# Scores of two heads on 64 rows each, and units taken in pairs, in the masked attention of a four-layer kernel

## The reference, cut to what matters

```python
def _masked_attention(xf, Wq, Wk, Wv, lookahead):
    q = jnp.einsum('bnd,hed->bhne', xf, Wq)
    k = jnp.einsum('bnd,hed->bhne', xf, Wk)
    v = jnp.einsum('bnd,hed->bhne', xf, Wv)
    scale = 1.0 / jnp.sqrt(jnp.asarray(q.shape[-1], q.dtype))
    s = jnp.einsum('bhqe,bhke->bhqk', q, k) * scale
    n = s.shape[-1]
    i = jnp.arange(n)
    mask = i[:, None] <= i[None, :] if lookahead else i[:, None] >= i[None, :]
    s = jnp.where(mask, s, jnp.finfo(s.dtype).min)
    p = jax.nn.softmax(s, axis=-1)
    return jnp.einsum('bhqk,bhke->bhqe', p, v)

o_lb = _masked_attention(xf, Wq_lb, Wk_lb, Wv_lb, lookahead=False)
o_la = _masked_attention(xf, Wq_la, Wk_la, Wv_la, lookahead=True)
o = jnp.concatenate([o_lb, o_la], axis=1)
out = jnp.einsum('bnd,od->bno', o.reshape(B, T * F, D), Wo)
```

## Time and profile before

| | |
|---|---|
| time, median of 3 runs (lowest, highest) | 1525.02 us (1522.62, 1526.16) |
| span of the profiled execution | 1518.8 us |
| PE busy | 1399.6 us, 92% of the span |
| DVE, ACT, POOL busy | 700.1, 390.7, 527.4 us |
| mean granted TensorE clock | 0.969 of full |
| one step of a pair in the second layer, looking back | 48.57 us |
| the same, looking ahead | 49.04 us |

### The profile page before, as it was taken

How to read it: one execution, slowest core, us unless ns; L and a number is a source line. 1 busy time by engine, 2 the same in 40 slices (tenths; PEclk the granted TensorE clock), 3 DMA queues, 4 the chain that set the end, 5 groups by cost and what they waited for, 6 DMA issues and landing times. The chain is left out here.

```text
span 1518.8 us, 20095 instructions
## 1 busy us (share of the span) xinstructions
PE 1399.6 (92%) x7344; PEld 1090.4 (72%) x7344; DVE 700.1 (46%) x1399; ACT 390.7 (26%) x941; POOL 527.4 (35%) x491
## 2 busy tenths in 40 slices
PE   4899799779999999999888999999999999795998
PEld 3678665358888877888666778777877787574787
DVE  6214423775345412455436555455234645558322
ACT  2311112043223301233201333233013322305322
POOL 3444298023332285223247322322442222144000
PEclk9899999899999999999989999999999999896999
DMA  4111052001111022111012101101110010000012
GB/s 172 42 42 42 28 85 36 0 28 40 38 32 31 28 76 63 35 28 35 28 42 82 35 22 35 29 27 27 42 41 28 28 35 28 15 28 3 0 35 77
DMA packets 36748, 59.63 MB, mean 39 GB/s; under 512 B 4848, under 2 KB 13840, under 8 KB 36688
## 3 DMA queue, kind: packets, MB, share of 16 engines
q1 hardware_dynamic: 35120, 55.42, 13.3%
q10 hardware_dynamic: 1568, 3.38, 0.6%
HBM read 50.40 MB, written 4.19 MB: 36 GB/s over the span
## 5 line engine op out<-in xcount | busy, mean ns | idle before, releaser
L127 POOL TENSOR_TENSOR w_hi<-w_raw,zeros 128x512 fp32r<-128x512 f32 x168 | 216.8, 1291 | 765.6 <-PE PS L151 731.8
L151 PE MATMUL PS<-xh,w_hi 128*128 128x512 f32 x960 | 332.9, 421 | 26.7 <-ACT xh L292 13.7
L151 PE MATMUL PS<-xl,w_hi 128*128 128x512 f32 x960 | 310.0, 397 | 3.0 <-DVE xl L286 2.7
L151 PE MATMUL PS<-xh,w_lo 128*128 128x512 f32 x960 | 309.4, 396 | 0.0
L129 POOL TENSOR_TENSOR w_lo<-w_raw,w_hi 128x512 fp32r<-128x512 f32 x168 | 220.1, 1310 | 13.2
L151 PEld LDWEIGHTS PS<-xh,w_hi 128*128 128x128 f32 x960 | 173.8, 192 | 69.5 <-issue 26.1
L151 PEld LDWEIGHTS PS<-xl,w_hi 128*128 128x128 f32 x960 | 181.8, 190 | 47.4 <-DVE xl L286 6.9
L151 PEld LDWEIGHTS PS<-xh,w_lo 128*128 128x128 f32 x960 | 182.9, 191 | 41.0
L1013 ACT ACTIVATE prob<-PS,nmax 128x256 f32<-128x256 f32 (+1 forms) x256 | 112.1, 443 | 229.3 <-DVE nmax L1142 114.9
L1154 DVE TENSOR_SCALAR prob<-prob,prec 128x256 f32<-128x256 f32 (+1 forms) x256 | 113.5, 485 | 4.5
L151 PE MATMUL PS<-oh,w_hi 128*128 128x512 f32 x256 | 93.4, 406 | 5.6 <-DVE ol L1087 3.7
(11 more groups left out here) (149 smaller groups left out, 1980.6 us busy)
## 6 DMA issues: line engine op xcount, KB each, us to landing
w_raw<-in_w SPq DMA_DIRECT2D x168, 256.0 KB, 2.6
A<-G SPq DMA_DIRECT2D x32, 128.0 KB, 4.5
out_x<-xT SPq DMA_DIRECT2D x16, 256.0 KB, 2.1
xT<-in_x SPq DMA_DIRECT2D x4, 512.0 KB, 8.3
xT<-in_x ACTq DMA_DIRECT2D x4, 512.0 KB, 8.7
ET<-in_emb ACTq DMA_DIRECT2D x1, 961.0 KB, 13.3
ka<-in_hot SPq DMA_DIRECT2D x2, 192.0 KB, 4.0
c<-in_c SPq DMA_DIRECT2D x1, 192.0 KB, 2.5
```

Of the source, the lines that this page charges most:

```text
L127: pool.tensor_tensor(w_hi[:, s, :], w_raw[:, s, :], zeros[:, :], ALU.add).then_inc(w_hi_done, 1)
L151: m = nc.tensor.matmul(PS[:, banks[h], :], wt[:, slot, w], x[:, c, h * HALF:h * HALF + HALF], start=first and k == 0, stop=last and k == 2)
```

## The change

The scores of both heads of an image are issued together, by a new function `scores_of_both`: for each of the two query blocks and each of the three products one matmul on rows 0 to 63 for the first head and one on rows 64 to 127 for the second, in turns, into bank S and bank S+1; then the four mask matmuls over all 128 rows, two into each bank, after which each bank's unit is reported. The queries have no padding and no planes any more: one ACT and one DVE instruction of 128 partitions each fill `qh` and `ql`, and the four memsets are gone.

The order in which PE goes through the units is new as well (`heads_in_pairs`). Before, scores and transposes alternated unit by unit. Now it is, for each image: scores of both heads, a chunk of v, transposes of the previous image's first head, a chunk of v, transposes of its second head, and outputs two images back. As both score banks are written at once, the scores of an image wait until ACT has taken the exponentials of both heads of the image before (`p_exp`). On DVE the first group of outputs leaves PSUM after unit 6 rather than 5. ACT's order keeps as it was.

```diff
@@ query tiles, evacuation on ACT and DVE
-            qh = sb(ctx, "qh", [P, 2, T], F32R)
-            ql = sb(ctx, "ql", [P, 2, T], F32R)
+            qh = sb(ctx, "qh", [P, T], F32R)
+            ql = sb(ctx, "ql", [P, T], F32R)
...
-                        for hh in range(2):
-                            rows = slice(64 * hh, 64 * hh + 64)
-                            last = nc.scalar.activation(qh[rows, hh, :], PS[rows, 0:2, :].rearrange("p a n -> p (a n)"), ACT.Copy)
-                        last.then_inc(q_evac, 1)
+                        nc.scalar.activation(qh[:, :], both, ACT.Copy).then_inc(q_evac, 1)
...
-                    if c in (4, 5) and masked:
-                        t = (qh, ql)[c - 4]
-                        nc.vector.memset(t[64:P, 0, :].bitcast(F32), 0.0)
-                        nc.vector.memset(t[0:64, 1, :].bitcast(F32), 0.0).then_inc(zeroed, 1)
...
-                        if u == 5:
+                        if u == (6 if masked else 5):
                             evac_o(j, int(ahead), 0)
@@ scores on PE
-                            for i, (x, y) in enumerate(((qh, kh), (qh, kl), (ql, kh))):
-                                nc.tensor.matmul(PS[:, S + u % 2, at + lo:at + hi], x[:, hh, qs], y[:, ks],
-                                                 start=i == 0, stop=False)
+                def scores_of_both(j, b, ahead):
+
+                    if b:
+                        pe.wait_ge(p_exp, 8 * j + 2 * b)
+                    for qt, (lo, hi) in enumerate(spans(ahead)):
+                        at = qt * N
+                        qs, ks = slice(b * N + qt * P, b * N + qt * P + P), slice(b * N + lo, b * N + hi)
+                        for i, (x, y) in enumerate(((qh, kh), (qh, kl), (ql, kh))):
+                            for hh in range(2):
+                                rows = slice(64 * hh, 64 * hh + 64)
+                                nc.tensor.matmul(PS[:, S + hh, at + lo:at + hi], x[rows, qs], y[rows, ks],
+                                                 start=qt == i == 0, stop=False, skip_group_check=True)
+                    for hh in range(2):
+                        for qt in range(2):
+                            at = qt * N + qt * P
+                            m = nc.tensor.matmul(PS[:, S + hh, at:at + P], identb[:, :], maskb[:, int(ahead), :],
+                                                 start=False, stop=True, skip_group_check=True)
+                        m.then_inc(s_done, 1)
@@ the order of the units on PE
+                def heads_in_pairs(j, ahead, more, next_v, second_half):
+                    for b in range(B):
+                        if b == 0 or b == 2 and not more:
+                            halves = 2 if more or b else 1
+                            pe.wait_ge(k_evac, 2 * j + halves)
+                            pe.wait_ge(split_done, 2 * j + halves)
+                        scores_of_both(j, b, ahead)
+                        if b == 0:
+                            next_v(1)
+                            next_v(2)
+                            second_half(range(0, 6))
+                            pe.wait_ge(v_ready, j + 1)
+                        else:
+                            next_v(2 * b + 1)
+                            if b == 1:
+                                second_half(range(6, CK))
+                            transposed(j, 2 * b - 2, ahead)
+                            if b < 3:
+                                next_v(2 * b + 2)
+                            transposed(j, 2 * b - 1, ahead)
+                            if b >= 2:
+                                outputs(j, 2 * b - 4, ahead)
+                    if not more:
+                        for u in (6, 7):
+                            transposed(j, u, ahead)
+                            outputs(j, 2 * u - 8, ahead)
```

More of the change, by code:

```diff
@@ L1091, in take_q @@
                     if masked:
-                        for hh in range(2):
-                            rows = slice(64 * hh, 64 * hh + 64)
-                            last = nc.vector.tensor_tensor(ql[rows, hh, :], PS[rows, 0:2, :].rearrange("p a n -> p (a n)"),
-                                                           qh[rows, hh, :].bitcast(F32), ALU.subtract)
-                        last.then_inc(qa_evac, 1)
+                        nc.vector.tensor_tensor(ql[:, :], PS[:, 0:2, :].rearrange("p a n -> p (a n)"), qh[:, :].bitcast(F32),
+                                                ALU.subtract).then_inc(qa_evac, 1)
                     else:
@@ L1226, in scores @@
                         qs, ks = slice(b * N + qt * P, b * N + qt * P + P), slice(b * N + lo, b * N + hi)
-                        if not masked:
-                            m = nc.tensor.matmul(PS[:, S + u % 2, at + lo:at + hi], q[:, hh, qs], k[:, hh, ks],
-                                                 start=True, stop=True)
-                        else:
-                            for i, (x, y) in enumerate(((qh, kh), (qh, kl), (ql, kh))):
-                                nc.tensor.matmul(PS[:, S + u % 2, at + lo:at + hi], x[:, hh, qs], y[:, ks],
-                                                 start=i == 0, stop=False)
-                            m = nc.tensor.matmul(PS[:, S + u % 2, at + qt * P:at + qt * P + P], identb[:, :],
-                                                 maskb[:, int(ahead), :], start=False, stop=True)
-                    m.then_inc(s_done, 1)
+                        m = nc.tensor.matmul(PS[:, S + u % 2, at + lo:at + hi], q[:, hh, qs], k[:, hh, ks],
+                                             start=True, stop=True)
+                    m.then_inc(s_done, 1)
+                def scores_of_both(j, b, ahead):
[15 more added lines that the diff above has]
+                        m.then_inc(s_done, 1)
                 def transposed(j, u, ahead):
@@ L1319, in step @@
                     next_v(0)
+                    if masked:
+                        heads_in_pairs(j, ahead, more, next_v, second_half)
+                        return
                     if not masked:
```

## The result

The changed kernel takes 1555.97 us, the median of 4 runs (1551.58 to 1560.2), against 1523.82 of 4 runs of the kernel before beside it: a ratio of 1.0214, 95% interval 1.019 to 1.0238. It is slower, by 32 us, where 26 were forecast. The time lies 5 us above the predicted 1551 and inside the range of 1532 to 1577.

A forecast was written before the change was run, and what follows sets the result against it. PE's matmuls bound the kernel before; a closed chain through ACT and DVE would afterwards. Looking back 16.4, looking ahead 10.9, last pair +1.6 - 1.1, start -1.35: +26.5 on 1518.8, 1545.3; median 6.2 above, 1551, range 1532 to 1577.

The forecast's parts named there:

- The closed chain: Second layer: from one image's scores through transposes, copy-out, exponentials and maxima to the next's, 6.77 us, so PE waits.
- The +2.7 us a step: Second layer, first score to last transposes of a step: 28.45 us instead of 25.77, before POOL's hold.
- little else: Kernel before: PE waits seven times for the copy of v, 4.0 us together, and hardly for anything more.
- The row halves: Scores: 64-row matmuls of both heads run at once; 1.14 us against 1.69, with 0.10 us drains at shape changes.
- The objection weighed ahead: Score weight loads: a load costs by its columns, not its rows, so 64 rows gain only by overlap.
- What DVE hid: DVE's scalings, slowed beside POOL, enter the chain: five a step, 1.4 us, range 0 to 4.
- The clock: Granted clock stays at 1.00 in the layer; rival: it falls once a step, 28 us more, 1579 us, chance 0.09.
- The start: Before the second layer's scores: dropping the memsets, which delay DVE about 3.6 us, removes PE's 1.35 us wait at 332.31.
- the wait at 736.36: Last step: filling the queries with one 128-partition instruction frees PE's wait of 1.06 us there.
- the last stretch: Last pair: no v chunk in the chain, 5.3 us per image against 4.5, twice: +1.6 us.
- No overlap: Rival at the scores: row halves don't run at once, 22 us more, 1573 us; chance 0.19.
- That PE keeps the pace: Rival: the wait at each image's first score falls within PE's own 4.7 to 5.8 us; 1501 us, chance 0.08.

The follow-up runs named there:

- e9: The changed kernel, but POOL's two weight splits write 32 of 512 columns from the second layer's third block on (products wrong): 1532.79 us.
- e10: The kernel before, but POOL's two weight splits write 32 of 512 columns from the second layer's third block on (products wrong): 1506.83 us.
- e1: The kernel before with only the new order of units and the wait for both heads' exponentials; padded queries and 128-row scores kept: 1576.08 us.
- e5: The changed kernel with DVE taking the maxima of both heads before the first head's scaling: 1510.51 us.
- e6: The changed kernel with both heads' maxima first on DVE, both transposes directly behind the scores, first outputs leaving PSUM after unit 7: 1493.61 us.
- e4: The kernel before, its order unchanged, with unpadded queries and each unit's six score matmuls on its own head's 64 rows: 1530.93 us.
- e8: The orders of e6 on PE and DVE, with the padded queries and 128-row scores of the kernel before: 1512.78 us.
- e3: The changed kernel with the first head's six score matmuls ahead of the second head's six, instead of in turns: 1571.45 us.
- e2: The changed kernel with the transposes of the previous image's first head directly behind the scores, ahead of the chunk of v: 1542.93 us.

## Why the prediction was right, and where its size was off

**The closed chain** held, link by link. Forecast from the first to the second image's scores 5.09 us, measured 5.09 (409.70 to 414.79). Forecast 6.77 from one image to the next, measured 6.70 (422.13 to 428.83), and 6.70 in e9 for the other one. Forecast for the stretch from the first score to the last transposes 28.45 and 1.4 for POOL, measured 29.48 (409.70 to 439.18). The idle times before the scores were said to be 1.2, 2 and 1 us; they are 0.99, 2.56 (1.93 without POOL) and 1.08, and the wait at unit 7's transposes is there. The +2.7 us a step stands by itself in e9 against e10: 51.25 against 48.59, 2.66. e1, which adds the order alone, and e5 and e6, which open the chain, show that it is the cause and not merely found beside the loss. One reading ahead was short: beside the waits for v, "little else" left out 7.6 us that PE waited for scaled probabilities, in 8 waits of up to 2.9, most of it in the last pair. There the kernel before wasn't paced by PE either.

**The row halves** overlap, as forecast. Two halves start within 4 ns, and the scores of both heads end 0.60 us earlier, forecast 0.55. The pause at the change of shape is there too: 0.21 us from the last score to the first mask (422.80 to 423.01), of which the score's own 256 columns take 0.11 (an estimate from the 512-column matmuls of L151, which start 0.23 apart), so about 0.1, as in the earlier trace rows. The objection weighed ahead, that fewer rows make nothing cheaper, holds where a 64-row matmul stands alone (e4); the gain is that of the overlap (e6 against e8). Turns aren't needed for all of it, since head 1's matmuls started ahead of three of head 0's in e3.

**What DVE hid** came out at its size. The forecast was 1.4 us a step and nothing in the kernel before; e9 gives 1.31 and e10 nothing in the looking-back steps. It was priced at the mean over all scalings. In the trace it is not a mean but two hits a step, each of 0.6 to 0.7.

**The clock** is the term that was mis-sized. The forecast held 1.00 in the layer at 0.91 and left the falls to a rival of 28 us at 0.09. They came, at a third of its price. The trace has a fall of 3.4 us in four steps and one of 6.8 in the first; the steps with a short one are 1.46 and 1.52 us longer than their neighbours (54.02 against 52.56, 53.91 against 52.39), the first one 2.46. With 1.5 for each of the two whose neighbours differ in work, that is 8.4 us (falls in the last pair, where PE idles in both kernels, aren't in it). The argument against it was that idle stretches of 1.06 us and more had left the clock at full. But the wait forecast for the third image was 2 us, and with POOL's share it was 2.56, longer than any of those. I should have followed my own two terms, 2.0 and 1.4, into one place. The trace of the kernel before also had a nearer case: PE waited 2.9 us up to 764.21, and from 766 to 772 the granted clock was already 0.51; the earlier trace rows show only what came later.

**The start** gave 0.37 us instead of 1.35 in these two traces. The memsets are gone, but DVE's instructions moved up beside POOL's splits. DVE of the changed kernel:

```profile
325.52 2.34 DVE L286 TENSOR_TENSOR xl<-ytmp,xh 128x1024 fp32r<-128x1024 f32 x1 [1.40 <-ACT xh L292]
328.00 2.50 DVE L267 TENSOR_SCALAR ytmp<-xT,coef 128x256 f32<-128x256 f32 x2
```

POOL's splits ran beside them from 325.49 for 1.29 us and from 326.93 for 2.06. The first takes 1.2 us elsewhere and the second about 0.74, so 2.9 of the 3.6 us saved went here, and PE's next matmul came at 331.68, 0.63 earlier than at 332.31. Over all runs a term of this size can't be told: the first score of the layer stands anywhere from 354.4 to 360.0 us, latest (358.0 and more) in e1, e3, e4, e5 and e8, where the granted clock was at its lower level for 10 us or more between 310 and 341, against 3.4 in the two traces compared here.

**The sum.** Forecast were 27.85 us for the eight steps (16.4, 10.9 and 0.5) and -1.35 for the start. Measured were 33.72 and -0.37. Without the 8.4 of the clock the steps come to 25.3: 15.7 looking back (16.4), 8.0 looking ahead with the wait at 736.36 gone (10.9 less 1.1), 1.6 in the last stretch (1.6, but in part by luck: the mean granted clock there was 0.82, against 0.91 before, a difference that the forecast didn't have). So the terms of the chain add up to 2.5 less than forecast, the clock to 8.4 more, and the start to 1.0 more. Behind the layer 2.35 us were saved that no term had: the same instructions ran at a mean granted clock of 0.97 instead of 0.96, within what that stretch varies by. 27.85 - 2.5 + 8.4 - 0.4 - 2.35 = 31.0, the growth of the span. That the total came within 5 us is luck in part, for what the clock took was met by two terms of 2.4 the other way.

**The rivals.** No overlap is excluded by the row pairs. That PE keeps the pace is excluded by 37.2 us of waits. Its price of 1501 is near what a kernel costs in which the chain is open (e6, 1493.61), but e6 has 12 us from its orders that this price didn't hold, part of them its waits for v.

## What to carry to other kernels

Before two units are merged to make an engine's work cheaper, follow the round trip from one issue of the unit to the next through every other engine, in each one's own order: here 0.6 us saved a pair met a chain that had become 1 to 2 us longer than PE's work. If such a chain closes, look for an instruction in it that nobody waits for. One exchange of two steps on DVE (both maxima ahead of the first scaling) turned 32 us of loss into 14 of gain, and moving the transposes (and the first outputs) made it 31. And price a stall together with what it may bring: two stalls that fall in one place make an idle time that neither makes alone. Here the clock fell in five of seven steps with an idle time of 2.55 us before the third image's scores, and in one of seven with 1.93.

## What the runs showed of the hardware

- Two fp32r matmuls of 128 or 256 columns on the two row halves start 3 to 4 ns apart behind a wait of PE, and some 30 ns apart without one; such pairs follow each other at 0.11 to 0.12 us (0.16 to 0.17 behind the first of a width), the pace of single ones of 64 rows.
- The halves overlap without taking turns too. With all six matmuls of one half ahead of the other half's in the program (e3), the second half's first started 0.01 us behind the first half's third, ahead of the first half's fourth, and the set took 0.29 us longer than in turns.
- Going into 64-row matmuls and back cost 0.17 us a unit in all (e4, a step of 8 units 49.97 us for 48.57).
- DVE's scaling from SBUF to SBUF is held beside POOL's splits in both of its forms, up to 2.64 us for 0.55 (e2) where two splits follow each other.
- Behind a PE wait of 2.55 us at 474.68 the granted clock was 0.51 for 3.4 us, although PE was busy for 88% of the step. A wait of the same length in the step before it, at 422.13, left the clock at full. So such a wait allows a fall and doesn't force one. With 1.93 us (e9) one step in seven had one, the first.
